# One engine's program as a loop: TensorE in the third edge stage of a four-layer graph network

## The reference, cut to what matters

```
emb = _radial_embedding(edge_length)
h = silu(emb @ mlp_w0 + mlp_b0)
h = silu(h @ mlp_w1 + mlp_b1)
w = (h @ mlp_w2 + mlp_b2).reshape(-1, 4, MUL)
ss, vv = xs[senders], xv[senders]
m0 = w[:, 0] * ss
m1 = w[:, 1][:, :, None] * ss[:, :, None] * Y1[:, None, :]
m2 = w[:, 2][:, :, None] * vv
m3 = w[:, 3] * (einsum('emc,ec->em', vv, Y1) / SQ3)
msg_s = segment_sum(concat([m0, m3]), receivers)
msg_v = segment_sum(concat([m1, m2]), receivers)
```

## Time and profile before

| | |
|---|---|
| median of 3 runs | 11154.02 us (11152.67 to 11200.2) |
| profiled execution, its own time | 11197.17 us |
| its span, first to last instruction | 11195.4 us |
| mean granted TensorE clock | 0.783 of full speed |
| PE busy | 7512.2 us (67%), 45679 matmuls, as many weight loads |
| DVE busy | 6853.5 us (61%) |
| POOL busy | 7061.2 us (63%) |
| ACT busy | 4365.1 us (39%) |

### The profile page before, as it was taken

How to read it: one execution, slowest core, us unless ns; L and a number is a source line. 1 busy time by engine, 2 the same in 40 slices (tenths; PEclk the granted TensorE clock), 3 DMA queues, 4 the chain that set the end, 5 groups by cost and what they waited for, 6 DMA issues and landing times. The chain is left out here.

```text
span 11195.4 us, 158258 instructions
## 1 busy us (share of the span) xinstructions
PE 7512.2 (67%) x45679; PEld 5676.2 (51%) x45679; DVE 6853.5 (61%) x18737; ACT 4365.1 (39%) x7367; POOL 7061.2 (63%) x6167
## 2 busy tenths in 40 slices
PE   1333333335899998998956777777777677777775
PEld 1322322333666666666645666666666344444443
DVE  3555555566677777666655666666666444444445
ACT  1111121121667776666621111111111566666664
POOL 3666666662688888888855555556554655555554
PEclk5555555556889999999977888888888788888887
DMA  4434434442666666777761111111111111111111
GB/s 118 110 96 105 111 98 104 101 97 65 103 106 106 107 106 109 109 109 109 110 117 46 43 43 43 43 42 43 42 42 46 45 43 44 44 44 45 44 44 43
DMA packets 1068830, 846.48 MB, mean 76 GB/s; under 512 B 404136, under 2 KB 907183, under 8 KB 1067542
## 3 DMA queue, kind: packets, MB, share of 16 engines
q0 software_dynamic: 360512, 407.88, 20.9%
q1 hardware_dynamic: 676812, 313.54, 12.7%
q10 hardware_dynamic: 30652, 115.04, 3.1%
HBM read 696.14 MB, written 139.60 MB: 75 GB/s over the span
## 5 line engine op out<-in xcount | busy, mean ns | idle before, releaser
L1474 POOL DMA_INDIRECT sums<-sumrows,index x1460 | 2458.1, 1684 | 694.3 <-issue 348.9
L1623 POOL DMA_INDIRECT rows<-table,index x1612 | 1583.8, 982 | 1128.8 <-DVE mid L1680 582.1
L679 POOL DMA_INDIRECT rows<-table,index x1612 | 1609.3, 998 | 1015.9 <-issue 692.0
L1873 POOL DMA_INDIRECT ACC<-table,index x1472 | 1398.4, 950 | 1129.2 <-DVEq L1998 615.1
L1650 DVE TENSOR_TENSOR ACC<-ACC,psS 128x256 f32 x1612 | 674.6, 418 | 792.1 <-PE psS L1714 471.2
L1714 PEld LDWEIGHTS psS<-hot,mid 128*128 128x128 f32 x6448 | 1042.9, 230 | 57.7 <-issue 3.0
L1714 PE MATMUL psS<-hot,mid 128*128 128x128 f32 x6448 | 1032.2, 313 | 2.7 <-DVE mid L1680 2.3
L2045 PE MATMUL psG<-limbs,pickA 128*128 128x384 bf16 x4060 | 902.1, 355 | 159.4 <-issue 102.7
L1910 ACT ACTIVATE pickA<-apart,K 128x512 bf16<-128x512 bf16 x1015 | 721.2, 711 | 717.2 <-remote 475.0
L1966 DVE TENSOR_TENSOR pickD<-ACC,psK 128x512 bf16<-128x512 f32 x700 | 459.9, 682 | 746.4 <-remote 545.4
L1421 PE MATMUL psB<-pickD,limbs 128*128 128x512 bf16 (+1 forms) x2964 | 824.5, 391 | 81.5 <-DVE pickD L1288 77.0
(11 more groups left out here) (349 smaller groups left out, 15303.0 us busy)
## 6 DMA issues: line engine op xcount, KB each, us to landing
win<-table SPq DMA_DIRECT2D x1612, 64.5 KB
srow<-src_f SPq DMA_DIRECT2D x365, 256.0 KB
HN<-rel_f ACTq DMA_DIRECT2D x102, 512.0 KB
relB<-rel_f ACTq DMA_DIRECT2D x102, 512.0 KB
rows<-table,index POOLq DMA_INDIRECT x3224
er<-limbs SPq DMA_DIRECT2D x1632, 3.0 KB
ACC<-table,index POOLq DMA_INDIRECT x1472
sums<-sumrows,index POOLq DMA_INDIRECT x1460
```

Source lines behind the costliest of these rows:

```text
L679: nc.gpsimd.indirect_dma_start(out=rows[:, r, k, :], out_offset=None, in_=table0[:, :], in_offset=bass.IndirectOffsetOnAxis(ap=index[:, n ...
L1474: nc.gpsimd.indirect_dma_start(out=sums1[u][:, :], in_=sums[:, n % 2, u, :], in_offset=None, compute_op=ALU.add, out_offset=bass.IndirectO ...
L1623: nc.gpsimd.indirect_dma_start(out=rows[:, n % R, u, :], out_offset=None, in_=table2[:, :], in_offset=bass.IndirectOffsetOnAxis(ap=index[: ...
L1873: nc.gpsimd.indirect_dma_start(out=rows[:, n % R, u, :], out_offset=None, in_=table3[:, :], in_offset=bass.IndirectOffsetOnAxis(ap=index[: ...
```

## The change

PE's program in the third edge stage calls `ring` where it called `straight`. Two groups' `radial` stand ahead of it as before. Steps 0 to 399 become 100 turns of a loop on TensorE with four steps in it; steps 400 to 402 are written out. The buffers' numbers in the loop are plain numbers still, and the values that PE waits for are computed from the turn's number in registers. The other engines' programs are not changed.

```diff
                             radial(0, 0, 0)
                             radial(1, 0, 1)
-                            straight(EDGE_GROUPS, R, step)
+                            ring(pe, EDGE_GROUPS, R, step)
```

## The result

The changed kernel takes 11,215.42 us (median of 12 runs, 11,200.2 to 11,248.09), the kernel before, run beside it, 11,178.77 us (12 runs, 11,147.02 to 11,202.04). The ratio is 1.0041 with a 95% interval of [1.003, 1.0053]: 46 us slower (34 to 59); the two medians lie 37 us apart. That is inside the half per cent that I called no change, and yet clear of the noise. The profiled execution took 11,231.25 us.

The account below looks back on a forecast made before the run. The third edge stage was taken as bound by a cycle of POOL's gathers and late signals, not one engine. Fetches 0, registers 0, branches 0, rest 0 to 50 us on the 11,154.0 median gave 11,165; eight-in-ten range 10,900 to 11,380.

Parts of the forecast that it names:

- The cycle: Third edge stage: fast groups make POOL gather without pause, PE's signals come late, its clock drops; average 6.71 us a group.
- Fetches of code: TensorE's queue q8: packets fall from 368 to about 275; gain put at 0, bound 90 us.
- that rival: Code fetches were the lateness: removing them gives up to 90 us and more, 11,060; chance 0.06.
- Branch and bookkeeping: PE's back edge, 33 + 45 + 50 ns and gaps, 99 times, hidden inside 0.41 us: 0, bound 30 us.
- That the body misses: Loop body of about 267 instructions refetched each turn: 11,320, at most 11,434; slower by the miss, chance 0.30.
- The price put on a miss: Exposure at each back edge: 2.8 us a turn (280 us) at most; about 1 us, 100 us, taken.
- a turn's pause: About 1 us once in four groups, partly given back by the cycle: net 0 to 50 us.
- the likeliest case's own: Range of the likeliest case for the whole kernel, 11,100 to 11,210 us; that forecast's chance 0.46.
- Register work: Computed wait values on PE, seven operations, 0.23 us a group: covered, so 0, bounded by 92 us.
- Those behind it run while PE works on L1699 and L1700: Register operations behind the wait for `mid` are covered by 0.8 us of PE's work before the first sum.
- I expect half to all of the pause to be given back.: Cycle's answer to a turn's pause of about 1 us: net 0 to 0.5 us a turn.
- the faster rival: PE slowed in every group breaks the cycle, POOL pauses in each: 407 us, 10,747; half broken 10,950; chance 0.18.

Follow-up runs that it names:

- nogather: Kernel before, POOL gathering only the first four groups' rows, used for all groups: 10,296.68 us, 0.9221; same edit on the changed kernel: 10,306.96 us, 0.924 (late chip).
- pause_land: Kernel before, POOL's gathers waiting until the previous group's rows landed: 10,311.64 us, 1.0891; same edit on the changed kernel: 10,289.27 us, 1.0869 (quiet chip).
- pause_memset: Kernel before, POOL filling an unread tile and waiting before each group's gathers: 1.0508 (quiet chip), 0.9837 (late chip); on the changed kernel 1.0514 (quiet chip).
- nops: Kernel before, written out, plus one TensorE no-operation between each group's waits and its first matrix: 9,461.6 us, ratio 1.0 (quiet chip).
- turn32: Changed kernel's TensorE loop with turns of 32 groups instead of four, 19 groups written out behind: 9,468.69 us, 1.0002 (quiet chip).

## Why the prediction was right, and where it was not

**What bounds the stage.** The cycle was right. On a late chip, take the gathers away and the late signals of this stage go with them; cut their rows to four with a pause and they go too, at 1.6% less time for more work. But it holds only there: two chips run endless rows with no late signal. The long row is a condition, not the cause. Why some chips send late signals stays open; what I have is that they also come in other stages (584 us of ScalarE's waits at L694, in the kernel before).

**Fetches of code.** Right: 277 packets against "about 275", and no gain. The late signals stayed with the fetches gone, so that rival falls.

**Back edge and the engine's memory.** Branch and bookkeeping were put at 0.2 to 0.3 us: 32 + 208 + 50 ns. That the body misses had a little better than even odds; it does not. The sentence of the Trainium skill on two pages (Runtime: NRT & Kernel Launch, Instruction fetch mechanics) was read too strongly in the prediction: a body of about 260 instructions need not leave two pages of 256. The price put on a miss, 2.8 us at the upper end, is what a real one shows (the product 2.8 us after `mid`). So the 0 to 50 us that the sum held for a turn's pause stood for something that does not exist. The forecast was 11 us over the median of before where 46 were measured, and its 0 to 50 is near that for a reason not its own: that part is luck. The measured 11,215 lies inside the eight-in-ten range, and 5 us outside the likeliest case's own (11,100 to 11,210); the kernel before, in its twelve runs, is itself 25 us above the three that the forecast stood on.

**Register work.** This is the term that was mis-sized: "So 0, bounded by 0.23 x 400 = 92 us". The count and the size were right (2,700 operations of 32 to 51 ns, 93 us in all), and nearly all of it is covered. The step that failed is the sentence on those behind the wait: "Those behind it run while PE works on L1699 and L1700". In two of four steps one operation, the fused one of L1698, stands between the wait and L1699. Nothing covers it, and the runs without gathers show its price: the groups that have it are 0.055 to 0.069 us slower than written out, those that don't are 0.017 us faster, 9 us in all of the 11. The same alternation, 0.13 to 0.15 and 0.05 us from `mid` to the product, is in the loops with a pause on POOL, where it costs nothing, because POOL sets the pace.

**What the cycle does with a delay.** "I expect half to all of the pause to be given back." The wrong way round, as the prediction named for its simplest error. Where nothing is late, the loop costs +10 us (nogather), -22 (pause_land), +6 within noise (pause_memset, across two chips). Where signals are late, it costs 37, 47 and 41 us by the medians (46, 50 and 31 by the ratios). So some 30 us come only where signals are late: that is shown by the pairs. How they come is argued. In each late pair the "remote" waits of the two silus rise, from 152 and 164 to 192, 197 and 204, which fits a delay that tips more groups into the slow kind, but such counts also wander in a stage that nobody touched. Late signals and a lower clock go together (0.82 here, 1.00 without gathers), and no pair parts them. A written-out kernel with a delay of its own at the head of each group, on a late chip, would be the test; `nops` was meant for it and delayed nothing.

**What should stay.** POOL's pauses were to stay at 188 and went to 234, with the mean clock at 0.82, not above 0.83: more pauses, as in the faster rival, but I read them as the echo of late groups, since the stage got slower and the clock did not rise. The faster rival's mechanism is real all the same: the memset's pause sets it off and got 189 of the 407 us, since with it a group takes 6.2 us and not 5.7.

## What to carry to other kernels

Turning an engine's written-out program into a loop cost little by itself here: 32 ns for a computed wait, 0.2 us for a turn, as long as the turn stays in the engine's memory. Look at the packets of the instruction queue and at the branch's own row. But look also at what stands between the wait that sets the pace and the first instruction behind it: a register operation there is covered by nothing, and it can stand in some steps of a turn and not in others, so look at the steps one by one, not at a row's mean. And where a stage lives in a cycle of fast and late groups, price a small delay with a run, and measure on more than one chip before a pause or a loop is kept.

## What the hardware showed that I had not expected

- One and the same kernel takes 11,160 to 11,179 us on three occasions and 9,460 to 9,468 us on two chips, 15% less, with the same instructions and the same bytes; the mean granted clock is 0.78 and 0.85. Beside it the traces show "remote" waits on the one kind and none on the other; this stage alone takes 2,706 us on a late chip and 2,022 on a quiet one, at a clock of 0.83 and 1.00.
- A backward branch on TensorE costs 0.21 us when the target is there and 3.3 to 3.9 us when it is not (3.52 in the median of turn32's row).
- Where the sequencer held the wait for VectorE, the first product started 0.10 us after the messages; where the product held it itself, 0.05 us; where a fused register operation of 37 to 51 ns stood between, 0.13 to 0.15 us. An added no-operation of TensorE in the same place made no difference (0.10 us).
